# A routed-expert kernel on one core: the order of the first routing and the place of the copy of x

## The reference, cut to what matters

```python
x = L0_attn_x                                   # 8 x 1024 tokens of 256 numbers: 8192 rows
x = x + 0.5 * ffn(layernorm(x))                 # first routed FFN ("a")
x = x + attn(layernorm(x))                      # the mixer
x = x + 0.5 * ffn(layernorm(x))                 # second routed FFN ("b")

def ffn(x):                                     # 16 experts, 2 per token, capacity 1280
    logits = x2d @ router_w.T + router_b
    vals, idx = top_k(logits, 2); gates = softmax(vals)
    pos = position of the choice in its expert, by a cumulative sum over all choices
    kept = pos < capacity; slot = expert * capacity + pos
    packed = zeros(16 * 1280 rows).at[slot].set(x)
    h = gelu(packed @ w1 + b1); out = h @ w2 + b2
    return sum over the two kept choices of gate * out[slot]
```

## Time and profile before

| | us |
|---|---|
| median of 3 runs | 3318.99 |
| the runs | 3316.73 to 3319.85 |
| the profiled execution, its own time | 3325.69 |
| its span (first to last instruction) | 3323.9 |

### The profile page before, as it was taken

The page is one execution under the profiler, slowest core; times in us unless marked ns, Lnnn a source line. Parts: engine busy times, 40 slices in busy tenths (PEclk is TensorE's granted clock), DMA queues, the critical chain, the costliest instruction groups (busy, mean ns, idle before and its releaser), DMA issues. The chain is left out here.

```text
span 3323.9 us, 63196 instructions
## 1 busy us (share of the span) xinstructions
PE 2899.8 (87%) x22656; PEld 2337.1 (70%) x22656; DVE 2005.2 (60%) x4425; ACT 1337.9 (40%) x2281; POOL 1695.3 (51%) x1510
## 2 busy tenths in 40 slices
PE   4453999999999995899999999974999999999997
PEld 4453888888888883466756666664888888888886
DVE  4343555555555653577888888753555555565563
ACT  3341444444444442343444444421444444444442
POOL 2543554554545443356676767644345445454543
PEclk9999999999999997899999999965999999999998
DMA  9813333343333324601111111002333334334334
GB/s 305 285 67 103 75 81 81 74 86 78 76 83 87 77 51 115 208 15 37 35 48 34 47 34 47 27 31 94 78 76 82 81 73 86 84 72 88 81 66 136
DMA packets 231849, 281.02 MB, mean 85 GB/s; under 512 B 18999, under 2 KB 214651, under 8 KB 231520
## 3 DMA queue, kind: packets, MB, share of 16 engines
q1 hardware_dynamic: 173760, 203.16, 20.3%
q0 software_dynamic: 57888, 75.16, 12.9%
HBM read 142.44 MB, written 146.41 MB: 87 GB/s over the span
## 5 line engine op out<-in xcount | busy, mean ns | idle before, releaser
L688 ACT ACTIVATE be_h<-be_pH,b 128x512 f32<-128x512 f32 (+1 forms) x384 | 237.2, 618 | 555.5 <-PE be_pH L623 483.1
L688 ACT ACTIVATE ae_h<-ae_pH,b 128x512 f32<-128x512 f32 (+1 forms) x384 | 237.2, 618 | 539.8 <-PE ae_pH L623 487.8
L714 POOL DMA_INDIRECT acc_a<-ae_ob,ae_to x160 | 254.9, 1593 | 94.1 <-POOL ae_ob L706 66.7
L706 POOL TENSOR_SCALAR ae_ob<-ae_ob,ae_gate 128x256 f32<-128x256 f32 x160 | 174.3, 1191 | 247.5 <-DVE ae_ob L829 247.5
L714 POOL DMA_INDIRECT acc_b<-be_ob,be_to x150 | 238.4, 1589 | 88.2 <-POOL be_ob L706 62.3
L706 POOL TENSOR_SCALAR be_ob<-be_ob,be_gate 128x256 f32<-128x256 f32 x150 | 163.0, 1183 | 222.4 <-DVE be_ob L829 222.4
L1461 POOL TENSOR_TENSOR m_xf<-m_tmp,m_xT 128x512 f32<-128x512 f32 x160 | 181.3, 1159 | 119.3 <-DVE m_tmp L1182 119.1
L434 POOL DMA_INDIRECT slots_a<-ar_row,ar_sidx x128 | 125.9, 984 | 158.7 <-issue 150.3
L1514 POOL DMA_INDIRECT slots_b<-m_row,m_sidx x128 | 152.9, 1195 | 84.0 <-issue 84.0
L1756 PEld LDWEIGHTS m_PP<-m_RP,m_KS 64*64 64x64 f32 x6656 | 121.1, 139 | 88.4 <-issue 87.3
L1756 PE MATMUL m_PP<-m_RP,m_KS 64*64 64x64 f32 x6656 | 135.7, 226 | 37.6 <-DVE m_A L1212 36.5
(11 more groups left out here) (342 smaller groups left out, 9384.7 us busy)
## 6 DMA issues: line engine op xcount, KB each, us to landing
ae_stage<-in_w SPq DMA_DIRECT2D x64, 512.0 KB
be_stage<-in_w SPq DMA_DIRECT2D x64, 512.0 KB
slots_a<-empty SPq DMA_DIRECT2D x10, 2080.0 KB, 19.7
ae_xp<-slots_a SPq DMA_DIRECT2D x80, 260.0 KB
slots_b<-empty SPq DMA_DIRECT2D x10, 2080.0 KB, 19.2
be_xp<-slots_b SPq DMA_DIRECT2D x80, 260.0 KB
ar_xin<-in_x SPq DMA_DIRECT2D x16, 512.0 KB, 5.8
acc_a<-ar_xin SPq DMA_DIRECT2D x16, 512.0 KB
```

The lines of the kernel that those rows point to most:

```text
L688: t = act.activation(dst[:, 0:SIZES[b]], pH[c % 2][:, 0:SIZES[b]], ACT.Gelu, bias=S.b1[:, bass.ds(i * (2 * FC) + (u * FC + f), 1)])
L706: t = pool.tensor_scalar(ob[m][:, q, :], ob[m][:, q, :], gate[m][:, q:q + 1], None, ALU.mult)
L714: pool.indirect_dma_start(S.acc[tag][:, :], bass.IndirectOffsetOnAxis(ap=to[m][:, q:q + 1], axis=0), ob[m][:, q, :], None, bounds_check=T ...
```

## The change

RING goes from 4 to 8. The logits run two steps ahead of `choose` (three buffers `pL`, `pC` only one, with the new semaphore `prefix_used`), and `assign(s)` stands ahead of `statistics(s+4)`. An empty-row DMA now covers two slabs: each partition writes two neighbouring rows, 2080 bytes in one piece, so there are five DMAs of twice the bytes, in both routings; each waits ahead of every second tile. The loads of groups 3 to 7 each have one such DMA behind them. `keep` is gone from the routing, with its semaphores. In its place `experts` "a" copies x from the input to `acc_a` with eight DMAs from memory to memory, 1 MiB each, and writes both sets of spare rows. SP issues these ten after the first expert's loads, ahead of the first weight part of the second expert, and POOL waits for all of them (`kept`) ahead of its first `send`.

```diff
@@ route @@
-        RING = 4
+        RING = 8
...
-        pL = [ps(f"pL{u}", [P, GQ, E]) for u in range(2)]
-        pC = [ps(f"pC{u}", [P, GQ, E]) for u in range(2)]
+        pL = [ps(f"pL{u}", [P, GQ, E]) for u in range(3)]
+        pC = ps("pC", [P, GQ, E])
...
-        STEPS = range(-3, NG)
+        STEPS = range(-4, NG)
...
-                for g in range(NG):
-                    if tag == "a":
-                        keep(g)
-                    if g + XRING < NG:
-                        load(g + XRING)
-                if tag == "a":
-                    for a in "ab":
-                        sp.dma_start(S.acc[a][T:, :].rearrange("(j p) d -> p j d", p=P),
-                                     S.empty[:, :, 0:D]).then_inc(S.spare_zeroed, 16)
...
+                for g in range(XRING):
+                    load(g)
+                    if XRING - PAIRS <= g:
+                        S.empty_rows(sp, tag, g - (XRING - PAIRS))
+                for g in range(XRING, NG):
+                    load(g)
...
                 for s in STEPS:
-                    if 0 <= s + 2 < NG:
-                        scale(s + 2)
+                    if 0 <= s + 3 < NG:
+                        scale(s + 3)
                     if 0 <= s + 1 < NG:
                         choose(s + 1)
-                    if s + 3 < NG:
-                        statistics(s + 3)
                     if s >= 0:
                         assign(s)
+                    if s + 4 < NG:
+                        statistics(s + 4)
...
                     pe.wait_ge(seen_ready, g + 1)
-                    pe.matmul(pC[u][:, :, :], S.before[:, :], cnt[u][:, :, :], start=True, stop=False)
+                    if g:
+                        pe.wait_ge(prefix_used, g)
+                    pe.matmul(pC[:, :, :], S.before[:, :], cnt[u][:, :, :], start=True, stop=False)
...
                 for s in STEPS:
-                    if 0 <= s + 2 < NG:
-                        turn(s + 2)
+                    if 0 <= s + 3 < NG:
+                        turn(s + 3)
                     if 0 <= s + 1 < NG:
                         prefix(s + 1)
-                    if 0 <= s + 2 < NG:
-                        logits(s + 2)
+                    if 0 <= s + 3 < NG:
+                        logits(s + 3)
...
-                        if g * GQ + q < SLABS:
-                            pool.wait_ge(S.emptied[tag][g * GQ + q], 16)
+                        if g * GQ + q < SLABS and q % 2 == 0:
+                            pool.wait_ge(S.emptied[tag][(g * GQ + q) // 2], 16)
@@ experts @@
+                if tag == "a":
+                    n = T // KEEPS
+                    for j in range(KEEPS):
+                        sp.dma_start(S.acc[tag][j * n:(j + 1) * n, :], S.x[j * n:(j + 1) * n, :]).then_inc(kept, 16)
+                    for a in "ab":
+                        sp.dma_start(S.acc[a][T:, :].rearrange("(j p) d -> p j d", p=P),
+                                     S.empty[:, :, 0:D]).then_inc(kept, 16)
...
+                        if tag == "a" and first and u == 0:
+                            pool.wait_ge(kept, 16 * (KEEPS + 2))
                         for m in units(0):
                             send(i, u, m)
@@ Shared @@
     def empty_rows(self, eng, tag, j):
 
-        slab = self.slots[tag].rearrange("(e j p) d -> j p e d", e=E, p=P)[j]
-        eng.dma_start(slab, self.empty[:, j, :].unsqueeze(1).to_broadcast([P, E, ROW])).then_inc(self.emptied[tag][j], 16)
+        slab = self.slots[tag].rearrange("(e j p r) d -> j p e (r d)", e=E, p=P, r=2)[j]
+        rows = self.empty[:, 2 * j:2 * j + 2, :].rearrange("p r d -> p (r d)")
+        eng.dma_start(slab, rows.unsqueeze(1).to_broadcast([P, E, 2 * ROW])).then_inc(self.emptied[tag][j], 16)
```

## The result

The changed kernel takes **3327.35 us** (median of 8 runs, 3324.06 to 3332.78) beside 3319.19 us for the kernel before: ratio 1.0027, 95% interval 1.0016 to 1.0038. I had forecast 3289.9 us, and the range of 3260 to 3304 doesn't hold it. It is slower, by some 8 us. The profiled execution took 3324.06 us, with a span of 3322.3 us.

What follows compares the result with a forecast made beforehand. The first routing was taken as bound by DMA until the last empty rows, then by POOL's scatters plus gaps. Routing -54.6 us and first expert +25.5 us gave -29.1, from 3318.99 to 3289.9 us; range 3260 to 3304.

Steps and rivals of the forecast that it cites:

- no ring wait is left ... POOL stays the bound: First routing after the empty rows: eight buffers end the ring wait, 111 scatters of 1.285 us run on to 231.6 us.
- The 9.2: First routing: a step supplying rows takes 9.2 us, against 10.3 us for POOL's eight scatters.
- 54.6 us: First routing: the last scatter's start moves from 286.20 to 231.6 us, a gain of 54.6 us (50.1 to 58.6).
- ACT's 40.2 us of waits for landing scatters: First routing: ACT's normalise waiting for one of four row buffers was read as causing POOL's 55 us of gaps.
- the gaps stay: Rival, first routing: gaps come from the step chain, not the row buffers; routing ends at 286.6, total 3344.9 us; 5%.
- everything behind it moves along: After the first routing: all later work starts earlier by the same 54.6 us as the last scatter.
- price: First expert: copies delay the second expert's weight part 0 and so DVE and PE, costing +25.5 us (+17 to +30).
- Empty rows in pairs: Start of first routing: pieces of 2080 bytes gain 4.5 us, the last empty rows land at 89.0 us (85.0 to 93.5).
- the straight line between small and large pieces: Empty rows: between 1040- and 4096-byte pieces, 2080 bytes give 379 GB/s, 8.5 us off; about half was taken.
- The prediction's estimate from the Trainium skill: Empty rows: fixed overhead of about 3 cycles per packet, so larger pieces gain some 4% or 2.7 us.
- The first rival: First expert: weights don't queue behind the copies, DVE doesn't stop, only the routing counts, 3264.4 us; 10%.
- the second (half rate): First expert: memory-to-memory copies run at 164 GB/s, DVE stops 25.6 us longer, 3315.5 us; 10%.

Runs made afterwards that it cites:

- e15: The changed kernel with its copies issued in the first routing and only the first choices' scatters there (64 in place of 128): 3228.89 us, one run.
- e3: The kernel before with eight row buffers instead of four, nothing else: 3332.68 us, ratio 1.0009.
- e2: The kernel before with only the copy part of the change, keep taken out and the ten copies in the first expert: 3353.21 us, ratio 1.0071.
- e1: The changed kernel with its ten copies issued in the first routing behind SP's loads, not in the first expert: 3308.58 us, ratio 0.9932 of before.
- e13: e1 unchanged, run again beside a kernel before of 3327.15 us: 3302.91 us, ratio 0.9929.
- e4: e1 with each of POOL's 128 scatters of the first routing replaced by an on-chip copy of 128x1024 numbers: 3256.57 us, one run.

## Why the prediction was wrong

**The step that failed** is "no ring wait is left ... POOL stays the bound": that once the buffers are enough, the supply of rows needs 9.2 us a step against POOL's 10.3. The 9.2 was right as a chain of work (8.77 us in e15), and on a prompt chip the changed kernel's scatters run without a gap as forecast (229.63 against my 231.6). But the kernel that I was given ran on a chip where signals come late during POOL's bursts, with waits of up to 21.9 us, and the supply fell behind POOL. There the last scatter started at 258.98, 27.4 us later than forecast. And on a prompt chip, where the forecast end comes true, the kernel before has no 55 us of gaps to lose: its last scatter is at 236.73. On neither kind can the change gain 54.6 us.

**The reading behind it.** I took ACT's 40.2 us of waits for landing scatters as the cause of the gaps. e3 took that wait away, and the four long gaps stayed to a tenth of a microsecond. It was a wait that ended beside the one that counted. The row that spoke against me was in rows 5: DVE's 14.62 us "remote", a wait whose other side the profile can't name. DVE needed PE's logits there, and in the same trace they were long done:

```profile
182.00 3.54 PE L379 MATMUL ar_pL<-rwT,ar_xT 128*128 128x16 f32 x16
...
199.61 0.59 ACT L408 COPY ar_xT<-ar_pT 128x512 f32<-128x512 f32 x1 [9.41 <-remote]
```

They ended at 185.54, 14.0 us before DVE began at 199.52. ACT too went on in that moment, 7.4 us after the transposes it needed had ended (192.23). No ring of buffers makes an engine wait for a result that is there. I explained it by ACT's lateness and gave the rival "the gaps stay" 5%. Of that rival the outcome was right in part (31 of 55 us stayed, past its point of 29), its mechanism, the length of the chain, was not.

**The sum, term by term**, late chip, traces: forecast -29.1; last scatter +27.4; the end of the routing +2.6, which I had left out ("everything behind it moves along"); price -2.1 (23.4 in place of 25.5): -1.2, and the two traces differ by 1.6. The median after lies 37.4 us above the forecast; the terms make 27.9 of it, and the other 9.5 lie between traces and medians. Before and after on the prompt chip give +20.2.

**Empty rows in pairs:** forecast 89.0 us (85.0 to 93.5), measured 85.13 and 86.94. From 20 to 85 us the DMA engines moved 375 GB/s against 329, 14% more (373 against 333 on the prompt chip, 12%), near the 379 of the straight line between small and large pieces; half of it was too little. The prediction's estimate from the Trainium skill, "DMA: Bandwidth & Descriptors", section Bandwidth, was some 4%; the measurement decides, and the gain of larger pieces was about three times that.

**The price:** right in mechanism and nearly in size. The chain of waits was as drawn; the queueing began earlier than I had it, since SP could issue the weight part only at 307.61, behind the last copy. The cast came 50.8 us after the stage's start in place of 19.7, 31.1 us later (forecast 33.6); DVE waited 25.5 us (28.2), PE 20.8 us (23.5), and the clock was low for 4.9 us (4). Whole, by the length of the stage: 23.4, 24.7 and, in e2, 24.8 us. The first rival (no queueing) falls; the second (half rate) falls too. From 278 to 288 us, with little but copies under way, the prompt chip moved 323 GB/s:

```profile
278.00:288.00 10.00, 0.00 (x0) 0.00 (x0) 0.00 (x0) 0.00 (x0) 0.00 (x0) 0.50 0.90 323
```

**What stays open.** What in a burst of scatters holds the signals up, and why on some chips only. Shown is that it goes with the chip or the occasion and not with the kernel, that it came with bursts of sixteen scatters or more and hardly with four or eight and a pause, and that the load of the DMA engines is no higher. Whether the number of scatters counts or their bytes is open: e7, e1 with a quarter of the bytes in each scatter, gave no measurement. Perhaps a sign of the same thing: for the scatters from 95 to 225 us the profile gives a median of 2.5 us from issue to landing on the prompt chip and finds none to give on the late one. It is open too how much the toll varies between executions of one kernel (e1 and e13, the same kernel on two late chips, start the experts at 270.44 and 264.56). With the scatter of the stages behind, such variation is the likely place of the 9 us between traces and medians of the first comparison; that is not shown.

## The better version

e1's kernel (the whole change, but with the copies of x issued in the routing behind the loads) beats before on either kind of chip: 0.9932, 0.9929 and 0.9978 of it. The changed kernel stands at 1.0027 and 1.0061. The differences are all under 1%, but clear of the noise. What lost time in the change is the place of the copies and, by 2.6 us, the eight row buffers. A smaller ring with the copies in the routing was not run.

## What to carry to other kernels

A releaser named in the profile is a candidate, not a cause: take its wait away alone (here one constant) before building a sum on it, and treat a wait with an unnamed other side as the first suspect. Before a stage's gaps are put down to the program, profile the same kernel on a second chip; here 50 us of 3320 came and went with it. Large copies that nobody waits for belong behind the last load of a stage whose DMA engines are idle, never ahead of the weights of the next stage on the same queue.

## What the runs showed of the hardware

- **The same kernel differs between chips (or occasions) in a way that the clock doesn't show.** With a granted clock of 0.96 on both kinds, the same kernel took 3274 to 3276 us on three occasions and 3319 to 3329 us on three. Nearly all of it (49.5 of 53.7 us between the two traces of before) lies in one stage, in which POOL issues 128 indirect DMAs in long bursts. The second routing issues as many, but four in a row between other work of POOL (seen from 1800 to 1900 us of before), and no "remote" wait stands out behind 300 us on either kind.
- **Signals between engines can come late beside bursts of indirect DMAs**, by up to 19.9 us (ACT's copy at 130.24 behind transposes that ended at 110.38), and DVE's wait for an instruction of its own is among them; in three gaps they were prompt again 1.7 to 2.7 us after the burst. Bursts of four with pauses of 3.9 us, or of eight with 2.4 us, leave at most a wait or two of 2 to 3 us.
- **A DMA behind large copies can hold its issuing engine:** behind some 10 MB of copies SP needed 21.87 us to issue the last one, the spare rows, in e2 (21.48 in the changed kernel).
- **Eight row buffers in place of four cost 2.6 us at the end of the stage** (6.11 us against 8.7 from the last scatter to the next stage's first issue, on both kinds of chip). POOL then waits for eight semaphores in place of four; that this is the reason is likely, not shown.
- **POOL's copies slow DVE:** beside them, some short DVE instructions took 0.5 to 1.1 us in place of 0.15 to 0.3 (e4).
